# Splitting the query table of a typed attention pass into two float32r halves, with the register loads of the work tables split in two

## What is computed

```python
q = typed_linear(x, Wq, bq).reshape(n, h, dk)
key_e = k_rel[edge_type, edge_src]
val_e = v_rel[edge_type, edge_src]
att = (q[edge_dst] * key_e).sum(-1) * rel_pri[edge_type] / jnp.sqrt(jnp.float32(dk))
seg = edge_dst * r + edge_type
...
hsum = jax.ops.segment_sum(w[:, :, None] * val_e, seg, num_segments=S)
```

## Time and profile before

| | us |
|---|---|
| median of 3 runs | 8832.05 |
| lowest, highest | 8828.82, 8837.01 |
| span of the profiled execution, first to last instruction | 8830.1 |
| TensorE matmul, busy | 6600.0 (75%) |
| VectorE, busy | 5164.4 (58%) |
| GpSimd, busy | 4060.3 (46%) |
| ScalarE, busy | 2234.7 (25%) |

### The profile page before, as it was taken

How to read it: one execution, slowest core, us unless ns; L and a number is a source line. 1 busy time by engine, 2 the same in 40 slices (tenths; PEclk the granted TensorE clock), 3 DMA queues, 4 the chain that set the end, 5 groups by cost and what they waited for, 6 DMA issues and landing times. The chain is left out here.

```text
span 8830.1 us, 116392 instructions
## 1 busy us (share of the span) xinstructions
PE 6600.0 (75%) x27378; PEld 5018.6 (57%) x27379; DVE 5164.4 (58%) x9644; ACT 2234.7 (25%) x4857; POOL 4060.3 (46%) x4373
## 2 busy tenths in 40 slices
PE   4977777774736666679999999974788885787886
PEld 2546566563525444546666666653676673666665
DVE  3138888886243333246666666665666666566666
ACT  1222222221310000123333333332333331333332
POOL 0025555552037777124444444423666661666663
PEclk9988888886857777589999999986777776677777
DMA  2247767666013333133343344332444441544443
GB/s 92 99 144 212 214 208 213 207 209 151 4 57 105 105 105 105 29 108 115 115 124 114 116 121 116 117 83 85 135 139 135 131 140 37 149 133 135 136 135 90
DMA packets 440058, 1096.42 MB, mean 124 GB/s; under 512 B 102452, under 2 KB 177296, under 8 KB 439410
## 3 DMA queue, kind: packets, MB, share of 16 engines
q0 software_dynamic: 249344, 763.23, 30.9%
q1 hardware_dynamic: 190180, 328.60, 11.1%
HBM read 1009.55 MB, written 81.94 MB: 124 GB/s over the span
## 5 line engine op out<-in xcount | busy, mean ns | idle before, releaser
L731 POOL DMA_INDIRECT st_rows<-g_table,st_stage_idx x1632 | 1558.0, 955 | 873.4 <-issue 463.6
L824 POOL DMA_INDIRECT st_rows<-kv_table,st_stage_idx x832 | 806.2, 969 | 671.1 <-PE st_psM L1167 391.2
L2385 PE MATMUL st_psM<-st_msg,st_hot 128*128 128x273 f32 x3264 | 942.6, 449 | 128.0 <-DVE st_msg L2233 102.6
L677 POOL DMA_INDIRECT st_rows<-p_table,st_stage_idx x816 | 854.3, 1047 | 302.9 <-issue 220.3
L731 POOL DMA_INDIRECT st_rows<-h_table,st_stage_idx x816 | 777.0, 952 | 244.5 <-issue 234.8
L2385 PEld LDWEIGHTS st_psM<-st_msg,st_hot 128*128 128x128 f32 x3264 | 702.9, 221 | 321.5 <-DVE st_msg L2233 91.2
L1519 DVE TENSOR_TENSOR st_pre<-st_psP,st_rows 128x512 f32<-128x512 f32 x816 | 523.5, 682 | 531.5 <-PE st_psP L1610 392.6
L1616 PE MATMUL st_psC<-st_w,st_rT 128*128 128x256 f32 x3264 | 814.7, 392 | 0.0
L1616 PEld LDWEIGHTS st_psC<-st_w,st_rT 128*128 128x128 f32 x3264 | 587.3, 190 | 373.7 <-ACT st_rT L1577 212.3
L1426 PE MATMUL st_psM<-st_rows,st_hot 128*128 128x256 f32 x1632 | 512.3, 484 | 372.5 <-DMA st_rows<-h_table,st_stage_idx 190.4
L1426 PEld LDWEIGHTS st_psM<-st_rows,st_hot 128*128 128x128 f32 x1632 | 401.3, 251 | 480.7 <-issue 331.3
(11 more groups left out here) (394 smaller groups left out, 11250.1 us busy)
## 6 DMA issues: line engine op xcount, KB each, us to landing
st_dst_row<-in_dst_row SPq DMA_DIRECT2D x310, 512.0 KB, 5.7
kv_table<-st_rows_out SPq DMA_DIRECT2D x25, 1560.0 KB, 5.7
st_ea<-in_ea SPq DMA_DIRECT2D x103, 256.0 KB, 3.8
st_rows<-g_table,st_stage_idx POOLq DMA_INDIRECT x1632, 2.8
st_pens<-pen_table SPq DMA_DIRECT2D x208, 72.0 KB
st_rows<-kv_table,st_stage_idx POOLq DMA_INDIRECT x832, 4.5
st_rows<-h_table,st_stage_idx POOLq DMA_INDIRECT x816, 2.7
st_rows<-p_table,st_stage_idx POOLq DMA_INDIRECT x816, 3.7
```

The costliest lines, as they stand in the source:

```text
L677: pool.indirect_dma_start(out=rows[:, u * SLOTS + j, :], out_offset=None, in_=table, in_offset=bass.IndirectOffsetOnAxis(ap=stage_idx[:, u ...
L731: pool.indirect_dma_start(out=rows[:, slot, j, :], out_offset=None, in_=table, in_offset=bass.IndirectOffsetOnAxis(ap=stage_idx[:, g, u * ...
L824: pool.indirect_dma_start(out=rows[:, slot, j, :], out_offset=None, in_=kv_table, in_offset=bass.IndirectOffsetOnAxis(ap=stage_idx[:, g, u ...
L2385: last = nc.tensor.matmul(out[:, 0:MSG_W], onehots[:, j, :], msg[:, n, j, :], start=(j == 0), stop=(j == SLOTS - 1))
```

## The change

The query table gets twice the columns: a high half (the queries rounded to float32r) and a low half (the query minus its high half). The product of a one-hot with the query rows becomes two products that add up in PSUM, both with float32r operands. The reading of the work tables is split in two: a load of the two counts, which now has its bounds checked at run time, and a load of the other two numbers, unchecked as before. This applies to `work_of` too, and so to all passes over edges.

```diff
-    q_table = dram("q_table", [NPAD + P, D])
+    q_table = dram("q_table", [NPAD + P, 2 * D])
...
+            q_low = st.sb("q_low", [P, NB, D], F32R)
+            q_high = NODE[:, :, 0:D].bitcast(F32R)
...
-                        sp.dma_start(q_table[ds(b * P, P), :], NODE[:, block_of(b), 0:D].squeeze(1)).then_inc(S["k_out"], 16)
-                        sp.wait_ge(S["k_out"], 32 * b + 32)
+                        sp.dma_start(q_table[ds(b * P, P), 0:D], NODE[:, block_of(b), 0:D].squeeze(1)).then_inc(S["k_out"], 16)
+                        sp.dma_start(q_table[ds(b * P, P), D:2 * D], q_low[:, block_of(b), :].squeeze(1).bitcast(F32)).then_inc(S["k_out"], 16)
+                        sp.wait_ge(S["k_out"], 48 * b + 48)
...
-                        v.tensor_copy(NODE[:, block_of(b), 0:D].squeeze(1), psY[:, 0:D]).then_inc(S["kv"], 1)
+                        v.tensor_copy(q_high[:, block_of(b), :].squeeze(1), psY[:, 0:D]).then_inc(S["halved"], 1)
+                        dve.wait_ge(S["halved"], START + b + 1)
+                        v.tensor_tensor(q_low[:, block_of(b), :].squeeze(1), psY[:, 0:D], NODE[:, block_of(b), 0:D].squeeze(1),
+                                        ALU.subtract).then_inc(S["kv"], 1)
...
     def work_of(eng, row):
+        _, counts = nc.values_load_multi_w_load_instructions(
+            work[0:1, ds(row, 1), 0:2].squeeze(1), engines=[eng.engine], min_val=0, max_val=NS * NB)
         _, values = nc.values_load_multi_w_load_instructions(
-            work[0:1, ds(row, 1), :].squeeze(1), engines=[eng.engine], min_val=0, max_val=NS * NB,
+            work[0:1, ds(row, 1), 2:4].squeeze(1), engines=[eng.engine], min_val=0, max_val=NS * NB,
             skip_runtime_bounds_check_because=BOUNDED)
-        return values
+        return (*counts, *values)
...
-            hotrow = st.sb("hotrow", [P, UT, SLOTS, P])
+            hotrow = st.sb("hotrow", [P, UT, SLOTS, P], F32R)
...
-            q_rows = st.sb("q_rows", [P, UT, D])
+            q_rows = st.sb("q_rows", [P, UT, 2, D], F32R)
...
                             for j in range(HALF):
-                                last = nc.tensor.matmul(psE[h][:, j * D:(j + 1) * D], onehots[0:NQ, h * HALF + j, :],
-                                                        queries, start=(fresh and j % 2 == 0), stop=True, skip_group_check=True)
+                                for n in range(2):
+                                    last = nc.tensor.matmul(psE[h][:, j * D:(j + 1) * D], onehots[0:NQ, h * HALF + j, :],
+                                                            queries[:, n, :], start=(fresh and j % 2 == 0 and n == 0), stop=True, skip_group_check=True)
```

## The result

The changed kernel takes 9635.8 us (median of 4 runs, 9627.1 to 9642.2) against 8833.7 for the kernel before beside it (8828.8 to 8837.0): a ratio of 1.0909, interval 1.0894 to 1.0924, 802 us more. I forecast slower, 9273, within 9000 to 9500. The direction held; the loss is nearly twice what I summed up and lies outside the range. The profiled execution has a span of 9634.7 us.

The account below looks back on a forecast made before the run. VectorE and its sequencer were taken to bound the typed pass. Typed pass 230, tables 11, edge MLP 80 and GAT 120 sum to 441 us, added to the median 8832: 9273 us, range 9000 to 9500.

Parts of the forecast that it names:

- dear bound of 1.42 us a read everywhere: All passes over edges: 0.726 us for a long second load plus six small instructions; 727 us in all, outside the range.
- What bounds the typed pass, and that the products change no end: Typed pass: VectorE and its sequencer set it, never waiting for an expand, so the float32r products bring no change.
- The price of a read, "0.9 us": Each work-table read: one added load of 0.34 us plus five small instructions of 0.115 us; bounds 0.34 to 1.42.
- 273 us against 230: Typed pass: five bare VectorE reads a group at 0.9 us, 4.5 us over 51 groups, 230 us (87 to 362).
- 146 against 80: Edge MLP: VectorE's read at supertile heads delays the end 89 times by 0.9 us, 80 us (30 to 126).
- The GAT layers, "120 us": GAT: ScalarE's three bare reads at a group's end add 2.7 us, in full for half the groups; 120 us (42 to 230).
- The tables, 11 us,: Tables: the subtraction reading PSUM holds the release of TensorE's transposes, 0.45 us in each of 25 blocks, 11 us.
- The weighted pass, nothing: Weighted pass: GpSimd issues gathers back to back and makes no such read, so no time is added.
- Free checks: Rival, all edge passes: checks cost no time and only the second load counts; 170 us more, 9002 us; chance 0.22.
- Free reads: Rival: the added reads cost nothing and only the tables' 11 us are left; 8843 us; chance 0.06.
- TensorE as the limit: Rival, typed pass: reads free and both expands halved on the path, 257 us less; 8586 us; chance 0.04.
- The cold scatter: Rival, typed pass: an idle gap leaves the scatter at 1.2 GHz throughout, 7.33 to 14.7 us; 71 us more, 9344; chance 0.11.

Follow-up runs that it names:

- one_load: The changed kernel, float32r halves kept, with every work row read by one load of four values and no bounds check; 8871.2 us, ratio 1.0046 to the kernel before.
- two_loads: The changed kernel with its two loads per read kept but no bounds check on the counts; 9162.9 us, ratio 1.0380 to the kernel before.

## Why the prediction was right or wrong

The stages lost 805 us where I had 441. Of the 364 that were missing, 160 are in GAT, 77 in the jump back of the typed pass, 66 in the edge MLP, 43 in the typed pass's reads and 18 in the tables. Even my dear bound of 1.42 us a read everywhere, 362 + 11 + 126 + 230 = 729 us by its terms, is below the 802 measured: the price of a read was not the only step that failed, but also which reads count, and the code's length.

*What bounds the typed pass, and that the products change no end:* right. VectorE never waited for an expand in the changed kernel, and one_load has the pass at its old length with expands that take 60% of the time.

*The price of a read, "0.9 us", failed for the reads that use all four numbers.* It was a sum of one load at its known 0.34 us and five small instructions. The small ones were right in size: two checks take 0.55 us. The load was wrong: splitting it made both halves slower than the whole, 0.53 each. A read whose four numbers are used became 2 x 0.53 - 0.34 + 0.55 = 1.27 dearer, and in the MLP's head more than that (1.57, with a register operation of 64 ns for the second address); one of counts alone became 0.53 - 0.34 + 0.55 = 0.74 dearer, its second load dropped (0.80 and 0.85 in the rows). I had taken 0.34 to 0.726 for the added load, and left the load that stays at its old price. In the typed pass this nearly evens out, 5.35 us a group against 4.5, 273 us against 230, inside the bounds. In the edge MLP, where every head reads all four, it does not: 146 against 80. My upper bound there, 126, was 1.42 at 89 heads. Over the whole pass VectorE's idle time at the heads went from 138.9 us at 91 of them to 303.0 at 101, 164 us, of which the pass shows 146.

*The loop's jump back was no step of mine.* 77 us of the typed pass's 352 are there. Nothing in the earlier trace rows hints at it, since the group's turn with the jump had 2.22 us against 1.94; but the kernel before has such pauses elsewhere, 3.48 us at each jump of VectorE's weighted loop and 3.27 in its GAT loop (medians). Anything that adds code to a loop has to be asked whether it brings one.

*The GAT layers, "120 us", the largest step that failed, and in three ways.* I priced three of ScalarE's nine reads a group and put the rest at nothing. I let ScalarE's added 2.7 us count in half the groups, and "VectorE's own four reads run mostly under products of 2.3 us: nothing"; TensorE's reads there I did not price at all. The runs give ScalarE 132 us over both layers (at least, as its pause came back in that run), VectorE 91, and TensorE and SyncE 80 once the others are relieved, 303 in sum where 280 were lost together.

*The tables, 11 us,* had the right mechanism: 0.57 us a block where I had 0.45, 24 x 0.57 = 14. Of the other 15 us, 14 are nine more blocks at a lower clock, each 1.4 to 1.7 longer.

*The weighted pass, nothing:* right, -1 us.

*The rivals.* Free checks fall: the changed kernel differs from two_loads by its checks, and is 473 us above it (77 of them the pause). Free reads fall: 402.0 us on issue. TensorE as the limit falls: one_load does not go below the kernel before. The cold scatter is half true. In one_load the scatter starts at 1317.66 behind 3.15 us of idle time, and takes 9.24 us instead of 7.33:

```profile
1317.66 9.24 PE L1176 MATMUL st_psM<-st_rows,st_hot 128*128 128x262 f32 x32 [3.15 <-DVE st_rows L1043]
```

The granted clock is 0.55 over its first 4.4 us and 1.00 after. It does not stay at 1.2 GHz throughout, as the rival had it, and the slack of 3.8 us covers the 1.9 while the reads stand at the turn. (The list of waits of one_load puts 81 of the 96 us ahead of that one-hot down to ScalarE's copies and to the scatter. But the one-hot waits only for the first of the two copies, which was done 3.7 us ahead of it in the median; the second ended while the reads ran, or, in 21 of 50 groups, later than the one-hot began.) The Trainium skill, page "TensorE: Matmul & The Clock Gate", section "HAM oscillation — how this bites in real kernels", describes a burst that begins at the low clock after a wait; the trace agrees with that, but in one_load it is no cost of the pass.

## What to carry to other kernels

Price a read of registers by its row, not by its bytes: here one load of four was 344 ns and each of two 530, and what it costs depends on what the engine has queued when the read comes, so read early, once, and behind long instructions. Before splitting or checking something in an inner loop, list for every engine of a chain which of its reads stand bare, also those ahead of work that looks idle. A gain on an engine that nobody waits for (206 us of TensorE here) is no gain, and can be paid back in clock.
